# A gated cross-attention and mixture-of-experts kernel: the expert stage in 25 tiles of 256 rows and 21 tiles of 128 rows in place of 39 tiles of 256

## The chip, the cores and the metric

The kernel runs on one core of one Trainium2 chip. The metric is the device time of one execution in microseconds (us), the median over several runs. Lower is better.

## What is computed

The input x holds 4 sequences of 1024 tokens with 256 numbers each; ctx_1024 holds 77 context rows for each sequence. The reference, cut to what matters:

```python
# x: (4, 1024, 256); 16 heads of 16; 8 experts, hidden width 1024, 2 experts for each token
x = x + tanh(g_xattn) * xattn(layernorm(x), ctx, ctx)      # scores are abs(q k) / 4, softmax, then Wo
xf = layernorm(x).reshape(-1, 256)
probs = softmax(xf @ w_router)
topk_w, topk_idx = top_k(probs, 2)
weights = sum(topk_w[..., None] * one_hot(topk_idx, 8), axis=1)
h = gelu(einsum('te,ieh->tih', xf, w1) + b1)               # 256 -> 1024 in each expert
out = sum((einsum('tih,ihe->tie', h, w2) + b2) * weights[..., None], axis=1)
x = x + tanh(g_ffn) * out
```

Only the two chosen experts of a token have to be worked out. That makes 4096 x 2 = 8192 rows of expert work, spread unevenly over the 8 experts by the data.

## The kernel before, in words

**Attention stage.** Tokens go in 16 pairs of tiles (256 rows) through layer norm, attention, the router and a scatter: each token's normalised row, its 8 expert weights and its number (265 numbers in all) are written to two places of a DRAM buffer `routed`, one in the region of each chosen expert. The regions have room for all rows, so the rows of an expert lie packed from the start of its region.

**The plan.** When the counts are known, VectorE works out a table for the tiles of the expert stage: `expert_of[tile]` and `row_of[tile]` (L1307 to L1360, some 20 small dependent operations, each with its wait on the semaphore `plan`; `planned` and L1109 to L1143 did the same for the first six tiles, `EARLY_TILES`, from a count taken earlier). A count of 256 rows per tile that does not come out even leaves a partly filled tile for each expert. So there are always 8192 / 256 + 7 = 39 tiles (`MAX_TILES`, L66), whatever the data; rows beyond an expert's end are padding (`pad_rows`, weight 0), and unused tiles point at a padding region.

**Expert stage.** Each tile of 256 rows goes through five engines, which are kept in step by semaphores (`ready` waits for a count; `settled` the same with a no-op):

- SP (`load_tile`, L651) reads `row_of` and starts the DMA of 256 rows into `x_row[:, pj]`, two buffers.
- PE (`turn_tile`, L1533) turns the rows with four transposes of 128x128 float32 into the bank `X_T`; ACT (`high_rows`) writes the float16 high part `x_hi`, DVE (`low_rows`, L1154) the rest `x_lo`.
- PE (`first_layer`, L1514): for each of 8 chunks of 128 hidden units and each of the 2 chunks of 128 inputs three products, w1_hi x_hi, w1_hi x_lo and w1_lo x_hi. So that is 48 matmuls, with 128x128 weights from w1 and 256 columns of rows moving. Two chunks share one of four PSUM banks (`HID_BANKS`).
- ACT (`gelu`, L872) applies bias and gelu, a chunk at a time; DVE (`split_hidden`, L1145) splits the result into h_hi and h_lo, two chunks at a time.
- PE (`second_layer`, L1542): for both halves of 128 rows and 8 chunks three products, again 48 matmuls. Here the hidden rows (128x128) are the loaded weights and 256 columns of w2 move.
- DVE (`finish_rows`, L1159) adds the bias and multiplies by weight and gate; POOL (L763) adds the 128 rows of each half to `out` with an indirect DMA. A tile's first one waits until those of the tile before have landed (L770). POOL also copies the weights and row numbers aside (`copy_meta`, L756), once the `added` count of two tiles before is there.

The order on PE is, for tile j: first layer of j, transposes of j+1, second layer of j-1 (`step`, L1555). `tile_pipeline` (L475) writes the first and last tiles out and runs the middle ones (8 to 35) in a loop. The expert of a tile is a number in a register, so `expert` (L594) loads it from the table at each use (L600), and the address of each weight slice is worked out in PE's own instruction queue, ahead of the matmul:

```python
                            for w, x in ((k.w1_hi, x_hi), (k.w1_hi, x_lo), (k.w1_lo, x_hi)):
                                mm = pe.matmul(
                                    H[:, q, c % PER * SLOTS:(c % PER + 1) * SLOTS],
                                    w[:, bass.ds(e, 1), i, c * P:(c + 1) * P].rearrange("p a n -> p (a n)"),
```

PE touches e with each (chunk, input chunk) of the first layer and each chunk of the second one. Waits on a semaphore stand in the same queue.

Of the kernel before, what the change touches and what calls it, by code (L numbers as in the profile page):

```python
# [22 lines left out]
F16 = mybir.dt.float16  # L23
BF16 = mybir.dt.bfloat16
I32 = mybir.dt.int32
# [40 lines left out]
MAX_TILES = TOKENS * 2 // SLOTS + E - 1  # L66
EARLY_TILES = 6
OWN_META = (2, 3, 4, 5)
EARLY_PAIRS = 10
LATE_TILES = MAX_TILES - EARLY_TILES  # L70
assert EARLY_PAIRS * 4 * 128 > (EARLY_TILES - 1) * SLOTS + E * (SLOTS - 1)
FULL_TILES = MAX_TILES - 2 * (E - 1)
# [68 lines left out]
def setup_phase(nc, t, k):  # L141

    banks = k.banks
    with ExitStack() as ctx:
# [17 lines left out]
        iota_j = sb("iota_j", [P, MAX_TILES + 1], I32)  # L162
# [26 lines left out]
        with nc.Block() as block:  # L189
# [75 lines left out]
            def _(pool):  # L265
# [20 lines left out]
                pool.iota(iota_j[:], pattern=[[1, MAX_TILES + 1]], base=0, channel_multiplier=0).then_inc(made, 1)  # L286
# [178 lines left out]

LOOP_TILES = range(8, MAX_TILES - 3 - (MAX_TILES - 3) % 2)
FULL_TILES_LOADED = 10
assert EARLY_TILES < LOOP_TILES.start and EARLY_TILES <= FULL_TILES_LOADED <= min(FULL_TILES, LOOP_TILES.start + 2)


def tile_exists(tile):
    return not isinstance(tile, int) or 0 <= tile < MAX_TILES

# [11 lines left out]

def main_phase(nc, t, k, out, routed):
# [5 lines left out]
    NT = LATE_TILES + 1  # L492
# [8 lines left out]
    with ExitStack() as ctx:  # L501
# [3 lines left out]
        def sem(name):  # L505
# [37 lines left out]
        packed_row, run_of, skipped, late, row_f, expert_f = (  # L543
            plan_place[:, NT * RUNS + i * NT:NT * RUNS + (i + 1) * NT] for i in range(6))
# [3 lines left out]
        early = sb("early", [P, E])  # L548
# [4 lines left out]
        hid = stage[:].rearrange("p a n -> p (a n)").rearrange("p (c n) -> p c n", c=HC)  # L553
        h_hi = prob[:].rearrange("p i n -> p (i n)").bitcast(F16)[:, 0:2 * HC * SLOTS].rearrange(
            "p (i c n) -> p i c n", i=2, c=HC)
        h_lo = k.v_area[:].bitcast(F16).rearrange("p (i c n) -> p i c n", i=2, c=HC)
# [28 lines left out]
        PLAN_OPS = 21  # L585
# [3 lines left out]
        added = [sem(f"added{i}") for i in range(2)]  # L589
        xt_done, x_hi_sb, x_lo_sb = sem("xt_done"), sem("x_hi_sb"), sem("x_lo_sb")  # L590
# [14 lines left out]
        def meta_of(j, pj):  # L605

            if isinstance(j, int) and j in OWN_META:
                return meta[:, j] if j < 4 else late_meta[:, j - 4]
            return meta[:, pj]

# [19 lines left out]
        with nc.Block() as block:  # L630
            @block.sync
            def _(sp):
# [22 lines left out]

                def step(m, par):
                    j, mj, pj = item(m, par, 2)
                    if isinstance(j, int) and j == FULL_TILES_LOADED:
                        sp.wait_ge(k.pads, 16 * (E + 1))
                    if tile_exists(j):  # L660
                        load_tile(j, pj)
                    if isinstance(j, int) and j == EARLY_TILES:
# [31 lines left out]
                for i in range(2):  # L694
                    sp.wait_ge(added[i], 16 * SB * ((MAX_TILES + 1 - i) // 2))

            @block.gpsimd
            def _(pool):
# [63 lines left out]

                def step(m, par):  # L763
                    j, mj, pj = item(m, par, -2)
                    if tile_exists(j):
# [5 lines left out]
                        for b in range(SB):  # L771
# [3 lines left out]
                                y[:, pj, b], None, compute_op=ALU.add).then_inc(added[pj], 16)  # L775
                    j, mj, pj = item(m, par, 0)
                    if tile_exists(j) and (not isinstance(j, int) or j not in OWN_META):
                        copy_meta(j, mj, pj)

# [20 lines left out]
            def _(act):  # L800
# [85 lines left out]

                def step(m, par):
# [5 lines left out]
                    j, mj, pj = item(m, par, 1)  # L893
                    if tile_exists(j):
                        high_rows(j)
# [74 lines left out]
            def _(dve):  # L970
# [203 lines left out]

                def step(m, par):
# [4 lines left out]
                    j, mj, pj = item(m, par, 1)  # L1180
                    if tile_exists(j):
                        low_rows(j)
                    j, mj, pj = item(m, par, -1)
                    if tile_exists(j):
                        finish_rows(j, mj, pj)

# [123 lines left out]
                dve.wait_ge(plan_consts, 1)  # L1310
                dve.tensor_scalar(packed_row[:], k.tile_no[:, 0:NT], float(SLOTS), run_base[:, 0:1], ALU.mult, ALU.add)\
                    .then_inc(plan_consts, 1)
                dve.memset(run_base[:, RUNS:RUNS + 1], float(E * REGION)).then_inc(plan_consts, 1)
                dve.wait_ge(count_ps, 1)
                dve.tensor_tensor(k.pad_at[:], ROUTE[:, 0:E], k.region_of[:], ALU.add).then_inc(plan, 1)
                dve.tensor_copy(count_i[:, 0], ROUTE[:, 0:E]).then_inc(plan, 1)
                dve.tensor_scalar(count_i[:, 1], ROUTE[:, 0:E], float(SLOTS - 1), None, ALU.add).then_inc(plan, 1)
                done(3)

                dve.tensor_scalar(tiles_i[:], count_i[:], SLOTS.bit_length() - 1, None, ALU.logical_shift_right)\  # L1320
                    .then_inc(plan, 1)
                done(4)
                dve.tensor_copy(run_length[:], tiles_i[:]).then_inc(plan, 1)
                done(5)
                dve.wait_ge(plan_consts, 3)
                dve.tensor_tensor(run_length[:, 1], run_length[:, 1], run_length[:, 0], ALU.subtract).then_inc(plan, 1)
                dve.scalar_tensor_tensor(run_base[:, E:RUNS], run_length[:, 0], float(SLOTS), k.region_of[:],
                                         ALU.mult, ALU.add).then_inc(plan, 1)
                done(7)
                dve.tensor_tensor(run_length[:, 0], run_length[:, 0], early[:], ALU.subtract).then_inc(plan, 1)  # L1330
                dve.tensor_tensor(jump[:], run_base[:, 1:RUNS + 1], run_base[:, 0:RUNS], ALU.subtract)\
                    .then_inc(plan, 1)
                done(8)
                dve.tensor_tensor(upto_runs, upto, lengths.unsqueeze(1).to_broadcast([P, RUNS, RUNS]), ALU.mult)\
                    .then_inc(plan, 1)
                done(10)
# [454 lines left out]
```

## Time and profile before

| | us |
|---|---|
| median of 3 runs (709.91 to 711.79) | 710.87 |
| the profiled execution's own time | 711.22 |
| its span in the profile | 709.5 |
| matmuls (PE) busy | 686.8 (97%) |
| weight loads (PEld) busy, beside the matmuls | 621.6 (88%) |
| VectorE (DVE) busy | 478.6 (67%) |
| ScalarE (ACT) busy | 339.3 (48%) |
| GpSimd (POOL) busy | 315.4 (44%) |

The profiled execution took 1.7 us beyond its span, which is time ahead of the first and behind the last instruction. The attention stage lasts until about 280 us, and the expert stage to the end. A matmul's record (273 ns for 256 columns) holds its way through the array, so matmuls overlap: the pace is the distance of starts. PEldq is PE's instruction queue, which works out addresses, loads registers and waits.

### The profile page before, as it was taken

What the parts mean: (1) busy time and instruction counts of PE and PEld (TensorE: products, weight loads), DVE (VectorE), ACT (ScalarE), POOL (GpSimd) and SP (SyncE); (2) the same over time, 40 slices, a digit from 0 to 9 for tenths busy, and PEclk for the clock granted to TensorE, in tenths of its full rate; (3) what the DMA queues carried; (4) which work ended last, traced back from release to release, by engine and by line L of the source; (5) the groups of instructions that cost most, each with busy time, mean ns of one, the idle gap of its engine ahead of it and who ended that gap; (6) DMA issues with size and microseconds to landing.
All of it is one profiled execution on the core that took longest, in us unless ns stands there. A gap on an engine that the chain in (4) does not pass through costs nothing.

```text
span 709.5 us, 21524 instructions
## 1 busy us (share of the span) xinstructions
PE 686.8 (97%) x6793; PEld 621.6 (88%) x6794; DVE 478.6 (67%) x1246; ACT 339.3 (48%) x708; POOL 315.4 (44%) x420
## 2 busy tenths in 40 slices
PE   8899999999999998999999999999999999999992
PEld 6799999999999987898998998998989989889882
DVE  5787888887887857786575565665755656557551
ACT  4677777777677655233243342332433423324330
POOL 7324676777765547825232232332322323323233
PEclk9999999999999999999999999999999999999997
DMA  5244545455444533373332332333323323233222
GB/s 192 64 135 135 163 138 175 149 159 178 155 131 156 167 128 120 94 175 44 55 47 45 48 52 51 45 52 54 45 45 51 49 51 45 46 59 45 48 31 30
DMA packets 53091, 64.78 MB, mean 91 GB/s; under 512 B 4577, under 2 KB 48743, under 8 KB 52903
## 3 DMA queue, kind: packets, MB, share of 16 engines
q1 hardware_dynamic: 38479, 44.89, 20.9%
q0 software_dynamic: 14448, 19.06, 16.3%
q8 instruction: 37, 0.61, 0.4%
q14 instruction: 23, 0.19, 0.1%
q10 hardware_dynamic: 104, 0.04, 0.0%
HBM read 38.34 MB, written 25.54 MB: 90 GB/s over the span
## 4 chain that ended last, share of the span: by engine, by line
PE 58%; POOL 2%; issue 1%; DMA 1%; DVE 0%; POOLq 0%; DVEq 0%
PE banks L1548 28%; PE banks L1526 27%; PE banks L1538 2%; POOL routed L752 1%; DMA out_dram<-prob_t,meta 1%; POOL l_exp L735 0%; POOLq L630 0%; POOL out_dram L773 0%; POOL rstd L708 0%; DVE prob_t L1167 0%; DVE prob_t L1171 0%; POOL neg_mean L705 0%; DVE best_i L1041 0%; POOL meta L761 0%; DVE chosen L1050 0%
## 5 line engine op out<-in xcount | busy, mean ns | idle before, releaser
L876 ACT ACTIVATE stage<-banks,bias_t 128x256 f32<-128x256 f32 x312 | 130.8, 470 | 267.6 <-PE banks L1526 267.6
L1526 PE MATMUL banks<-xn_t,w_hi 128*128 128x256 f16 x1248 | 207.9, 274 | 0.7 <-DVE xn_t L1156 0.6
L773 POOL DMA_INDIRECT out_dram<-prob_t,meta x74 | 117.9, 1593 | 186.1 <-DVE prob_t L1171 164.9
L1526 PE MATMUL banks<-xn_t,w_lo 128*128 128x256 f16 x624 | 170.6, 273 | 0.0
L1548 PE MATMUL banks<-w_hi,v_area 128*128 x624 | 170.1, 273 | 0.0
L1548 PE MATMUL banks<-w_hi,prob 128*128 x624 | 170.1, 273 | 0.0
L1548 PE MATMUL banks<-w_lo,prob 128*128 x624 | 170.1, 273 | 0.0
L1526 PEld LDWEIGHTS banks<-xn_t,w_hi 128*128 x1248 | 122.3, 98 | 15.5 <-issue 1.2
L1151 DVE TENSOR_TENSOR v_area<-stage,prob 128x512 f16<-128x512 f32 x156 | 108.5, 695 | 5.4
L1167 DVE SCALAR_TENSOR_TENSOR prob_t<-banks,arena 128x256 f32<-128x256 f32 x78 | 32.8, 421 | 114.1 <-PE banks L1548 112.0
L752 POOL DMA_INDIRECT routed<-row,pos x64 | 69.8, 1091 | 27.9 <-issue 14.3
L1149 DVE CAST prob<-stage 128x512 f16<-128x512 f32 x156 | 67.2, 431 | 21.7 <-ACT stage L876 19.0
L1457 PEld LDWEIGHTS banks<-v_area,prob_t 128*128 128x128 f32 x640 | 73.9, 192 | 4.3 <-DVE attn L1000 0.7
L1457 PE MATMUL banks<-v_area,prob_t 128*128 128x34 f32 (+1 forms) x640 | 77.2, 277 | 0.3 <-DVE attn L1000 0.3
L1526 PEld LDWEIGHTS banks<-xn_t,w_lo 128*128 x624 | 61.3, 98 | 7.3
L1548 PEld LDWEIGHTS banks<-w_hi,v_area 128*128 128x128 f16 x624 | 61.0, 98 | 7.1
L1548 PEld LDWEIGHTS banks<-w_lo,prob 128*128 128x128 f16 x624 | 61.0, 98 | 7.1
L1548 PEld LDWEIGHTS banks<-w_hi,prob 128*128 128x128 f16 x624 | 61.0, 98 | 6.7
L981 DVE TENSOR_REDUCE top<-prob 128x16 f32<-128x1232 f32 x32 | 45.9, 1434 | 26.7 <-ACT prob L804 26.7
L1438 PE MATMUL banks<-ident,prob 128*128 128x128 f32 x320 | 51.2, 274 | 0.1
L832 ACT ACTIVATE prob_t<-banks 128x512 f32<-128x512 f32 (+1 forms) x96 | 45.6, 537 | 6.5 <-PE banks L1443 4.9
L761 POOL COPY meta<-x_row 128x18 f32<-128x18 f32 x37 | 7.6, 205 | 79.4 <-DMA out_dram<-prob_t,meta 74.7
(218 smaller groups left out, 991.0 us busy)
## 6 DMA issues: line engine op xcount, KB each, us to landing
stage<-in_L_ffn_w_dram SPq DMA_DIRECT2D x32, 512.0 KB, 4.0
x_row<-routed SPq DMA_DIRECT2D x39, 265.0 KB, 2.8
x_in<-in_x_dram SPq DMA_DIRECT2D x16, 256.0 KB, 3.4
x_res<-in_x_dram SPq DMA_DIRECT2D x16, 256.0 KB, 3.8
out_dram<-x_res SPq DMA_DIRECT2D x16, 256.0 KB, 2.7
routed<-pad_rows SPq DMA_DIRECT2D x9, 265.0 KB, 3.5
out_dram<-prob_t,meta POOLq DMA_INDIRECT x74, 3.8
routed<-row,pos POOLq DMA_INDIRECT x64, 2.8
```

What stands on the lines that cost most here:

```text
L752: pool.indirect_dma_start(routed[:, :], bass.IndirectOffsetOnAxis(ap=pos[:, held, tile, choice:choice + 1], axis=0), row[:, held, tile], N ...
L773: pool.indirect_dma_start(out[:, :], bass.IndirectOffsetOnAxis(ap=meta_of(j, pj)[:, b, E:E + 1].bitcast(U32), axis=0), y[:, pj, b], None, ...
L832: act.activation(prob_t[:, first:first + n, :].rearrange("p c n -> p (c n)"), T[:, g, 0:n * P], ACT.Exp, scale=DH ** -0.5).then_inc(pt_sb, 1)
L876: ins = act.activation(hid[:, c], H[:, q, c % PER * SLOTS:(c % PER + 1) * SLOTS], ACT.Gelu_apprx_tanh, bias=k.bias_t[:, bass.ds(e * HC + c ...
L981: dve.tensor_reduce(top_part(i, 0), prob[:, i % 2, 0:SCORES].rearrange("p (h k) -> p h k", k=KEYS), AX.X, ALU.max).then_inc(top_sb, 1)
L1149: dve.tensor_copy(h_hi[:, pj, part], hid[:, part]).then_inc(h_hi_sb, 1)
L1151: dve.tensor_tensor(h_lo[:, pj, part], hid[:, part], h_hi[:, pj, part], ALU.subtract)\
L1167: dve.scalar_tensor_tensor(y[:, pj, b], Y[pj][:, b * D:(b + 1) * D], 1.0 / W_SCALE, b2_b[:, bass.ds(e, 1), :].rearrange("p a d -> p (a d)" ...
L1438: pe.matmul(T[:, g, c * P:(c + 1) * P], prob[:, i % 2, (first + c) * P:(first + c + 1) * P], k.ident[:], is_transpose=True, start=(c == 0) ...
L1457: mm = pe.matmul(V[:, first * VW:(first + n) * VW], prob_t[:, c, :], k.v_rows[:, b, c, 0:n * VW], start=(c == 0), stop=(c == PCH - 1), ski ...
L1526: mm = pe.matmul(H[:, q, c % PER * SLOTS:(c % PER + 1) * SLOTS], w[:, bass.ds(e, 1), i, c * P:(c + 1) * P].rearrange("p a n -> p (a n)"), ...
L1548: mm = pe.matmul(Y[pj][:, b * D:(b + 1) * D], h[:, pj, c, b * P:(b + 1) * P], w[:, bass.ds(e, 1), c, :].rearrange("p a n -> p (a n)"), sta ...
```

## The change

The expert stage has two sorts of tiles. The first 25 (`FULL_TILES`, 32 - 7) have 256 rows and go on as before, with the loop over tiles 8 to 21. Behind them come 21 tiles of 128 rows (`SMALL_TILES`, (8192 - 25 * 256) / 128 + 7), written out. The plan takes full tiles only from whole 256 rows of an expert and shares the rest out to small ones. For a small tile the row DMA has 128 rows with four buffers, there are two transposes, and one scatter. On PE the two layers alternate: chunk c of tile j's first layer (6 matmuls of 128 columns), then chunk c of tile j-1's second layer (3 matmuls of 256 columns), with the transposes of j+1 after chunk 3. The plan has 31 operations on the semaphore `plan` in place of 21, and a table of 40 late tiles in place of 34.

```diff
 SLOTS = 256
 SB = SLOTS // P
-MAX_TILES = TOKENS * 2 // SLOTS + E - 1
+FULL_TILES = TOKENS * 2 // SLOTS - (E - 1)
+SMALL_TILES = (TOKENS * 2 - FULL_TILES * SLOTS) // P + E - 1
+MAX_TILES = FULL_TILES + SMALL_TILES
...
-LOOP_TILES = range(8, MAX_TILES - 3 - (MAX_TILES - 3) % 2)
+LOOP_TILES = range(8, FULL_TILES - 3 - (FULL_TILES - 3) % 2)
...
-    NT = LATE_TILES + 1
+    NT = LATE_TILES
...
-        PLAN_OPS = 21
+        PLAN_OPS = 31
...
+                def load_small(t):
+                    before = t - 2 if t < FULL_TILES + 2 else t - 4
+                    p, h, b = small_turn(t)
...
+                    ready(sp, xt_done, before)
+                    ready(sp, meta_sb, before)
+                    at = sp.value_load(k.row_of[0:1, t:t + 1], min_val=0, max_val=E * REGION)
+                    sp.dma_start(k.x_row[:, p, b], routed[bass.ds(at, P), :]).then_inc(small_ld[p][b], 16)
...
+                def scatter_small(t):
+                    p, h, b = small_turn(t)
+                    if t == FULL_TILES:
+                        ready(pool, added[0], FULL_TILES // 2, 16 * SB)
+                    else:
+                        ready(pool, small_added[1 - p], small_turn(t - 1)[1], 16)
+                    settled(pool, y_sb, t, SB)
+                    pool.indirect_dma_start(
+                        out[:, :], bass.IndirectOffsetOnAxis(ap=small_meta(t)[:, E:E + 1].bitcast(U32), axis=0),
+                        y[:, p, 0], None, compute_op=ALU.add).then_inc(small_added[p], 16)
...
+                def gelu_small(t, e, q):
+                    ready(act, hid_ps, t, HID_BANKS, q + 1)
+                    ready(act, h_lo_sb, t - 1, HID_BANKS, q + 1)
+                    for c in range(PER):
+                        ins = act.activation(small_part(hid_flat, q)[:, c * P:(c + 1) * P], H[:, q, c * P:(c + 1) * P],
...
+                    elif small_exists(j):
+                        e = expert(act, j)
+                        for q in range(HID_BANKS):
+                            gelu_small(j, e, q)
+                            if q == 1 and small_exists(j + 1):
+                                high_small_rows(j + 1)
...
+                def finish_small_rows(t):
+                    p, h, b = small_turn(t)
+                    e = expert(dve, t)
+                    ready(dve, y_ps, t)
+                    if t < FULL_TILES + 2:
+                        dve.wait_ge(added[p], 16 * SB * len(range(p, FULL_TILES, 2)))
+                    else:
+                        dve.wait_ge(small_added[p], 16 * h)
...
+                        for q in range(HID_BANKS):
+                            split_small_hidden(j, q)
+                            if q == 1 and small_exists(j + 1):
+                                low_small_rows(j + 1)
...
+                dve.tensor_tensor(upto_eight, upto[:, 0:E, 0:E], run_length[:, 0].unsqueeze(1).to_broadcast([P, E, E]),
+                                  ALU.mult).then_inc(plan, 1)
+                done(6)
+                dve.tensor_reduce(run_end[:, 0:E], upto_eight, AX.X, ALU.add).then_inc(plan, 1)
+                done(7)
+                dve.tensor_scalar(run_end[:, 0:E], run_end[:, 0:E], float(LATE_FULL), None, ALU.min).then_inc(plan, 1)
...
+                def first_small(t, e, c):
+                    q = c // PER
+                    if c == 0:
+                        ready(pe, x_lo_sb, t)
+                    if c % PER == 0:
+                        ready(pe, hid_sb, t - 1, HID_BANKS, q + 1)
+                    hi, lo = (x[t % 2].rearrange("p (i n) -> p i n", i=KC) for x in (small_x_hi, small_x_lo))
+                    n = 0
+                    for i in range(KC):
+                        for w, x in ((k.w1_hi, hi), (k.w1_hi, lo), (k.w1_lo, hi)):
+                            mm = pe.matmul(H[:, q, c % PER * P:(c % PER + 1) * P],
+                                           w[:, bass.ds(e, 1), i, c * P:(c + 1) * P].rearrange("p a n -> p (a n)"),
+                                           x[:, i], start=(n == 0), stop=(n == 3 * KC - 1))
+                            n += 1
...
+                def turn_small(t):
+                    p, h, b = small_turn(t)
+                    ready(pe, small_ld[p][b], h // 2, 16)
+                    ready(pe, x_lo_sb, t - 1)
+                    for i in range(KC):
+                        mm = pe.transpose(X_T[:, i * P:(i + 1) * P], x_row[:, p, b, i * P:(i + 1) * P], k.ident[:])
+                    mm.then_inc(xt_done, 1)
+
+                def second_small(t, e, c):
+                    p = t % 2
+                    if c == 0:
+                        ready(pe, y_bias, t - 2, SB)
+                    if c % PER == 0:
+                        ready(pe, h_lo_sb, t, HID_BANKS, c // PER + 1)
+                    for n, (h, w) in enumerate(((small_h_hi, k.w2_hi), (small_h_hi, k.w2_lo), (small_h_lo, k.w2_hi))):
+                        mm = pe.matmul(Y[p][:, 0:D], h[p][:, c * P:(c + 1) * P],
+                                       w[:, bass.ds(e, 1), c, :].rearrange("p a n -> p (a n)"),
+                                       start=(c == 0 and n == 0), stop=(c == HC - 1 and n == 2))
...
+                    elif isinstance(j, int):
+                        if small_exists(j):
+                            e = expert(pe, j)
+                        if small_exists(j - 1):
+                            e_before = expert(pe, j - 1)
+                        for c in range(HC):
+                            if small_exists(j):
+                                first_small(j, e, c)
+                            if small_exists(j - 1):
+                                second_small(j - 1, e_before, c)
+                            if c == 3 and small_exists(j + 1):
+                                turn_small(j + 1)
```

## Rows read from the trace of the kernel before

**Rows 1.** Page: busy time of PE, and its granted clock in 40 slices.

```profile
PE 686.8 (97%) x6793; PEld 621.6 (88%) x6794; DVE 478.6 (67%) x1246; ACT 339.3 (48%) x708; POOL 315.4 (44%) x420
...
PEclk9999999999999999999999999999999999999997
```

**Rows 2.** Chain that ended last, from 639.97 us: start, us, what.

```profile
664.53 0.44 PE banks L1538 x4
664.97 5.24 PE banks L1548 x48
670.21 5.24 PE banks L1526 x48
...
686.37 5.25 PE banks L1548 x48
...
695.37 3.83 DMA out_dram<-prob_t,meta
...
701.57 1.86 POOLq L630
```

**Rows 3.** PE's queue by line: ns min/median/max, first to last start.

```profile
L1526 PEldq FUSED_REGOPS  x12: 46/46/46, 494.4 to 497.2; - x12
...
L1548 PEldq FUSED_REGOPS  x8: 46/46/46, 587.2 to 588.9; - x8
```

**Rows 4.** The same view around loads of a tile's expert.

```profile
L600 PEldq TENSOR_LOAD <-expert_of x1: 300/300/300, 684.3 to 684.3; - x1
...
L105 PEldq EVENT_SEMAPHORE  x1: 51/51/51, 684.9 to 684.9; - x1
...
L1548 PEldq FUSED_REGOPS  x8: 46/46/46, 685.0 to 686.8; - x8
...
L600 PEldq TENSOR_LOAD <-expert_of x4: 298/299/312, 673.8 to 689.5; - x4
```

**Rows 5.** The same view of L1548 and L1526, 309.6 to 691.7 us (35 tiles).

```profile
L1548 PEldq FUSED_REGOPS  x286: 46/46/46, 314.4 to 691.5; - x143
...
L1526 PEldq FUSED_REGOPS  x556: 46/46/46, 309.8 to 683.9; - x186
```

**Rows 6.** Timeline, attention stage: start, us, engine, instructions.

```profile
150.67 0.39 PE L1443 MATMUL banks<-top_t,spread_top 128*128 128x128 bf16 x4
...
150.56 0.32 PEld L1443 LDWEIGHTS banks<-top_t,spread_top 128*128 128x128 bf16 x4
```

**Rows 7.** Page, part 5 and 6: ACT, DVE and the scatters of the expert stage.

```profile
L876 ACT ACTIVATE stage<-banks,bias_t 128x256 f32<-128x256 f32 x312 | 130.8, 470 | 267.6 <-PE banks L1526 267.6
...
L1151 DVE TENSOR_TENSOR v_area<-stage,prob 128x512 f16<-128x512 f32 x156 | 108.5, 695 | 5.4
...
L1149 DVE CAST prob<-stage 128x512 f16<-128x512 f32 x156 | 67.2, 431 | 21.7 <-ACT stage L876 19.0
...
out_dram<-prob_t,meta POOLq DMA_INDIRECT x74, 3.8
```

**Rows 8.** Timeline of DVE and POOL from 690 us.

```profile
692.32 0.41 DVE L1171 TENSOR_SCALAR prob_t<-prob_t,meta,gates 128x256 f32<-128x256 f32 x1
...
693.50 1.57 POOL L773 DMA_INDIRECT out_dram<-prob_t,meta  x1 [4.16 <-DVE prob_t L1171]
...
701.87 1.55 POOL L773 DMA_INDIRECT out_dram<-prob_t,meta  x1 [0.30 <-issue]
```

**Rows 9.** Timeline of DVE and PEld, 298 to 321 us (the plan).

```profile
301.20 0.72 DVE L1341 TENSOR_TENSOR x_in<-tile_no,run_end 128x544 f32<-128x544 f32 x1
...
305.56 0.69 DVE L1156 TENSOR_TENSOR xn_t<-banks,xn_t 128x512 f16<-128x512 f32 x1 [0.92 <-ACT xn_t L885]
...
319.88 0.68 DVE L1156 TENSOR_TENSOR xn_t<-banks,xn_t 128x512 f16<-128x512 f32 x1
...
320.70 0.11 PEld L1526 LDWEIGHTS banks<-xn_t,w_hi 128*128 x2 [0.32 <-issue]
```

**Rows 10.** Windows: us, PE, PEld, DVE, ACT, POOL busy (x), PEclk, DMA share, GB/s.

```profile
140.00:170.00 30.00, 30.00 (x344) 28.01 (x343) 24.74 (x85) 22.57 (x42) 21.90 (x35) 1.00 0.51 161
```

More of the change, by code:

```diff
@@ L463, in _, with small_exists, small_turn @@
                     mm.then_inc(k.v_done, 1)
-LOOP_TILES = range(8, MAX_TILES - 3 - (MAX_TILES - 3) % 2)
-FULL_TILES_LOADED = 10
-assert EARLY_TILES < LOOP_TILES.start and EARLY_TILES <= FULL_TILES_LOADED <= min(FULL_TILES, LOOP_TILES.start + 2)
+LOOP_TILES = range(8, FULL_TILES - 3 - (FULL_TILES - 3) % 2)
+assert EARLY_TILES < LOOP_TILES.start and LATE_FULL >= 0 and FULL_TILES % 2 == 1
 def tile_exists(tile):
-    return not isinstance(tile, int) or 0 <= tile < MAX_TILES
+    return not isinstance(tile, int) or 0 <= tile < FULL_TILES
+def small_exists(tile):
+    return isinstance(tile, int) and FULL_TILES <= tile < MAX_TILES
+def small_turn(tile):
+    h = (tile - FULL_TILES) // 2
+    return tile % 2, h, h % 2
 def tile_pipeline(eng, step, first):
@@ L541, in main_phase @@
         past = plan_place[:, 0:NT * RUNS].rearrange("p (n r) -> p n r", r=RUNS)
-        packed_row, run_of, skipped, late, row_f, expert_f = (
-            plan_place[:, NT * RUNS + i * NT:NT * RUNS + (i + 1) * NT] for i in range(6))
+        packed_row, run_of, skipped, late, row_f, expert_f, halved = (
+            plan_place[:, NT * RUNS + i * NT:NT * RUNS + (i + 1) * NT] for i in range(7))
         upto, upto_runs = (x_norm[:, i].rearrange("p (n r) -> p n r", r=RUNS) for i in range(2))
@@ L552, in main_phase @@
             "p (c n) -> p c n", c=KC) for i in range(2))
[L553 to L556, printed above, removed]
+        hid_flat = stage[:].rearrange("p a n -> p (a n)")
+        hid = hid_flat.rearrange("p (c n) -> p c n", c=HC)
+        h_hi_flat = prob[:].rearrange("p i n -> p (i n)").bitcast(F16)
+        h_lo_flat = k.v_area[:].bitcast(F16)
+        h_hi, h_lo = (h[:, 0:2 * HC * SLOTS].rearrange("p (i c n) -> p i c n", i=2, c=HC) for h in (h_hi_flat, h_lo_flat))
+        small_h_hi, small_h_lo = (
+            [h[:, i * HC * SLOTS:i * HC * SLOTS + HC * P] for i in range(2)] for h in (h_hi_flat, h_lo_flat))
+        small_x_hi, small_x_lo = (
+            [x.rearrange("p c n -> p (c n)")[:, i * KC * P:(i + 1) * KC * P] for i in range(2)] for x in (x_hi, x_lo))
         y = prob_t[:].rearrange("p c n -> p (c n)")[:, 0:2 * SB * D].rearrange("p (i b d) -> p i b d", i=2, b=SB)
@@ L589, in main_phase @@
         added = [sem(f"added{i}") for i in range(2)]
+        small_ld = [[sem(f"small_ld{i}{b}") for b in range(2)] for i in range(2)]
+        small_added = [sem(f"small_added{i}") for i in range(2)]
         xt_done, x_hi_sb, x_lo_sb = sem("xt_done"), sem("x_hi_sb"), sem("x_lo_sb")
@@ L609, in meta_of, with small_meta @@
             return meta[:, pj]
+        def small_meta(tile):
+            p, _, b = small_turn(tile)
+            return meta[:, p + 2 * (1 - b), 0]
         def chunk_parts(turn):
@@ L1318, in _ @@
                 done(3)
-                dve.tensor_scalar(tiles_i[:], count_i[:], SLOTS.bit_length() - 1, None, ALU.logical_shift_right)\
-                    .then_inc(plan, 1)
[L1322 to L1327, printed above, removed]
+                dve.tensor_copy(run_length[:, 0], tiles_i[:, 0]).then_inc(plan, 1)
@@ new lines, in _ @@
+                done(8)
+                dve.tensor_copy(run_length[:, 0, 0:1], run_end[:, 0:1]).then_inc(plan, 1)
+                dve.tensor_tensor(run_length[:, 0, 1:E], run_end[:, 1:E], run_end[:, 0:E - 1], ALU.subtract)\
+                    .then_inc(plan, 1)
+                done(10)
+                dve.tensor_tensor(taken[:], run_length[:, 0], early[:], ALU.add).then_inc(plan, 1)
+                done(11)
+                dve.scalar_tensor_tensor(l_left[:], taken[:], -float(SLOTS), ROUTE[:, 0:E], ALU.mult, ALU.add)\
+                    .then_inc(plan, 1)
@@ new lines, in _ @@
+                dve.tensor_tensor(upto_eight, upto[:, 0:E, 0:E], run_length[:, 1].unsqueeze(1).to_broadcast([P, E, E]),
+                                  ALU.mult).then_inc(plan, 1)
+                dve.scalar_tensor_tensor(skip[:, E:RUNS], run_length[:, 1], -float(P), jump[:, E:RUNS], ALU.mult, ALU.add)\
+                    .then_inc(plan, 1)
+                done(19)
+                dve.tensor_reduce(run_end[:, E:RUNS], upto_eight, AX.X, ALU.add).then_inc(plan, 1)
+                done(21)
```

148 lines of the change are left out of this document (107 added, 41 removed).

## The prediction

> **What bounds the kernel now.** Read the page first: PE is busy for 97% of the span at full clock [rows 1]. Next comes the chain of waits. Through the expert stage it runs on PE alone: 0.44 us for four transposes, 5.24 us for 48 matmuls of one layer, 5.24 us for 48 of the other [rows 2]. A step is 10.92 us, and a matmul of 256 columns starts every 5.24 / 48 = 0.109 us. ScalarE, VectorE and the scatters have gaps beside that.
>
> The third view is PE's own instruction queue, and it matters most. It works out the addresses of the weight slices, in pairs of one FUSED_REGOPS and one ALU_OP, and a pair serves three matmuls. When the queue is not held up, 12 pairs of the first layer start within 2.8 us, with two waits of 0.1 us among them: (2.8 - 0.2) / 11 = 0.236 us a pair. 8 pairs of the second layer start within 1.7 us, 0.243 us each [rows 3]. I take 0.237. With 256 columns three matmuls last 0.327 us, so the queue stays ahead and its time is hidden. With 128 columns that cover goes.
>
> **What goes.** Steps 25 to 38 are replaced. Step 38 has no transposes, so from the end of step 24 (call it t) to the end of step 38 they take 14 x 10.92 - 0.44 = 152.4 us, up to 691.6 us [rows 2]. The span's end is 17.9 us later. Together it is 170.3 us from t, which is near 539.2 us.
>
> **What a small step streams on PE.** First layer: 48 matmuls of 128 columns. The attention stage has such matmuls with new 16-bit weights for each: four take 0.39 us with the last one's 0.219 us, so they start every (0.39 - 0.22) / 3 = 0.056 us [rows 6]. 48 x 0.056 = 2.7 us. Second layer: 24 x 0.109 = 2.6 us. Two transposes: 0.2 us. The sum is 5.5 us, half of a full step. 21 of them would be worth 10.5 full steps, and 3.5 steps or 38 us would be saved, if PE only streamed.
>
> **What a small step costs in PE's queue.** A full tile has 16 pairs in the first layer (556 in 35 tiles) and only 8 in the second (286 in 36): its second half of rows uses the same addresses again [rows 5]. A small tile needs as many, since it goes through all of both weights: 24 pairs x 0.237 = 5.69 us. To this come the loads of the expert from the table. From such a load's start (684.3) to the next instruction (684.9) it is 0.6 us, and over four of them 0.65 us is the best value [rows 4]. A small step has two, for tile j and once more for j-1: 1.30 us. A wait that stands alone takes 0.1 us (684.9 to 685.0) [rows 4]; where two waits meet, one stands alone: in the first layer, the second layer and the transposes, 0.32 us. The transposes' own dispatch I put at 0.05 us. The sum is 7.36 us, 1.8 us more than PE streams. So I expect the small steps to run at 7.35 us, at the pace of the queue. The alternation by chunks helps only in part: for a chunk the queue needs 3 x 0.237 = 0.71 us and PE 6 x 0.056 + 3 x 0.109 = 0.66 us.
>
> What is unsure is mainly the transposes' part: I have no view of it with a free queue. From below it is 0; from above it is another 0.3 us, since the queue was held up for so long about a full tile's four. I stay near the lower end, for a small tile has two. With the rounding of a pair (0.236 to 0.243) a step lies between 7.2 and 7.7 us.
>
> **The sum.** Step 25 has a small first layer alone and then the full second layer of tile 24. The queue gets to the load of the expert some 2.1 us before PE is done with the step ahead (last load 689.5 [rows 4], PE until 691.6 [rows 2]), so PE streams 2.9 us at once, waits until 3.4 us for the next load and addresses, and then streams 5.24 us: to t + 8.6. The queue is free at t + 6.5. Twenty steps (26 to 45) of 7.35 are 147.0 us; PE trails the last address by some 0.3 us. Tile 44's second layer ends at t + 153.8.
>
> The tail from there: gelu, split and expert load of tile 45 stand before tile 44's finish on VectorE. A gelu takes 0.47, a cast 0.43 and a subtraction 0.69 us at full size [rows 7]; from half of each I put the last scaling at 2.1 us. From a scaling's start to its scatter it is 1.2 us (692.3 to 693.5) [rows 8], to its landing 3.8 [rows 2, 7]; the last scatter starts 0.8 us later, as it waits for that landing, and the span ends 7.6 us after its start (701.9 to 709.5) [rows 8]. That is 15.5 us, and the end is at t + 169.3. Before it was t + 170.3. So 1.0 us is saved here.
>
> The plan: ten more dependent operations of some 0.2 us each, smaller ones in place of two of 0.42 us, and four passes over 640 numbers in place of 544, each of which took 0.72 us [rows 9] and will take 0.12 more. I count 2.2 us until the table is done. The next operation had waited 0.92 us for ScalarE, which absorbs as much. The rest, 1.3 us, goes on: VectorE works with hardly a gap up to the rows of tile 5 (319.88), for which PE already waited (0.32 us before the weight load at 320.70) [rows 9]. PE would be 1.3 us late there, and nothing gives this back.
>
> Costed at nothing: the row DMAs (128 rows, four buffers, a step of lead); ScalarE, 8 shorter gelus of at most 0.47 us and a copy, about 3.4 us in a step of 7.35; VectorE, four splits of half of 1.12 us and a finish, about 4.2 us; POOL, whose scatters wait for one another: 3.8 us to landing and 0.8 to the next start are 4.6 us, for which 5.5 would do too. If a step fell to 4.6 us, the scatters would be next. PE's waits on x_lo and h_lo come 1 us or more after these are written, and the wait on `pads` is long met.
>
> Net: -1.0 + 1.3 = +0.3 us. The profiled execution took 711.2 us, and the median is 0.35 us less: 710.87 + 0.3 gives **711.2 us**. About 0.3% (2.1 us) is what a measurement of this kernel can tell from no change; twenty steps of 0.1 us are as much. So the sign of a small effect is open.
>
> **A rule that speaks against the change.** Each weight load's record lasts 98 ns, but four of them start within 0.32 - 0.10 = 0.22 us and do not hold up the matmuls at 0.056 us [rows 6]. The Trainium skill, page "TensorE: Matmul & The Clock Gate", section "LDWEIGHTS (loading the stationary operand)", gives a load as its columns / 1.2, which is 107 ns for 128 columns; by it a small step would be 48 x 0.107 + 2.6 + 0.3 = 8.0 us, 13 us more over twenty steps. The same page's part on fast weight load says that 16-bit weights of 128 columns load about twice as fast. The first of these rules is the third rival below; that runs in the attention stage are of four only is what leaves it alive.
>
> **The rivals.** (1) PE streams without the queue holding it, because the compiled code has fewer address operations or they are hidden in another way. Steps of 5.5 us then: t + 8.6 + 110.6 + 15.5 = 134.7, 35.6 us less than before, with the plan 34.3: 676.6 us. For it speaks that the queue never held PE so far; against it the constant pace of [rows 3]. Chance 0.13. (2) In between, for instance one expert load or some of the addresses saved, steps of 6.4 us: 692 us. Chance 0.06. (3) Weight loads that hold up the small matmuls: if in runs of six a load has to end before the next can start, a step is 48 x 0.098 + 2.6 + 0.3 = 7.6 us on PE itself, and the queue's lead of 2.1 us and 2.0 us of step 25 are lost too: 5 + 2.1 + 2.0 less the 0.3 of trailing, with +0.3 some 9 us, 720 us. It decides from 94 ns a load on, for there 48 loads and the rest reach 7.35 us. Against it stand [rows 6]. Chance 0.08. (4) The queue needs more than my list: 7.65 us a step for transposes and waits that it stops at: 6 us more, 717 us. Chance 0.11. (5) My sum within 0.25 us a step: 706 to 716 us, 0.62. The clock should not fall: it stayed at 1.00, the 2.4 GHz level, through 140 to 170 us with shorter and sparser matmuls [rows 10].
>
> **The numbers.** Forecast 711.2. The range 700 to 722 leaves out (1), half of (2) and a little above. Of the 0.62 of my case, 0.17 are faster by over 0.3%, 0.31 within and 0.14 slower. With (1) and (2) faster is 0.36; with 0.03 of (4) the same is 0.34; slower 0.30.
>
> **What to look for after.** Small steps (starts of the first chunk) 7.35 us apart, from the end of tile 24 on, with PE's gaps at the expert loads and pairs of addresses 0.237 us apart without hold-ups; first-layer matmuls 0.056 us apart within a run of three and with gaps between; 24 pairs and two loads a step; 21 steps over about 155 us; PE's wait before tile 5 about 1.3 us longer. I am wrong if the steps are near 5.5 us, if the small matmuls start 0.1 us apart, if pairs are fewer than 24, or if waits for the scatters show on VectorE.

## The result and the profile after

The changed kernel takes 720.7 us (median of 4 runs, 718.6 to 721.5) where the kernel before took 710.4 us beside it: a ratio of 1.014, with a 95% interval of 1.011 to 1.016. It is slower by 10 us. 711.2 us had been forecast, with a range of 700 to 722. So the result lies in the range, but only 1.3 us below its upper end, and the likeliest case was too friendly: a ratio of about 1.00 was forecast, and a third of the chances stood for each sign.

The page after, with the lines that answer to [rows 1] and [rows 7]:

```profile
PE 670.6 (93%) x6947; PEld 596.3 (83%) x6948; DVE 471.7 (66%) x1307; ACT 344.5 (48%) x771; POOL 305.9 (43%) x420
...
PE   7899999999999998999999999999999888888883
...
PEclk9999999999999999999999999999999999999997
...
L951 ACT ACTIVATE stage<-banks,bias_t 128x128 f32<-128x128 f32 x168 | 52.7, 364 | 107.9 <-PE banks L1713 107.0
...
L1713 PE MATMUL banks<-xn_t,w_hi 128*128 128x128 f16 x672 | 77.0, 220 | 22.2 <-ACT stage L951 22.2
...
out_dram<-prob_t,meta POOLq DMA_INDIRECT x67, 3.8
```

PE has 16 us less to do, and the time is longer. The granted clock stayed at 1.00 in the stage of the small tiles (the column after POOL in the windows below). The eight slices of PE before the last are at 8 and not 9: PE idles in every small step. The windows show how much (PE, PEld, DVE, ACT, POOL busy, clock, DMA share, GB/s), first after, over the steps 25 to 45, then before, over the steps 25 to 38:

```profile
541.50:703.10 161.60, 138.24 (x1577) 113.85 (x1574) 85.60 (x232) 57.88 (x187) 41.01 (x44) 1.00 0.24 37
```

```profile
539.20:691.60 152.40, 152.40 (x1399) 137.19 (x1397) 92.64 (x181) 53.30 (x125) 47.15 (x42) 1.00 0.30 47
```

PE is busy for 138 of 161.6 us. The timeline shows where the rest lies: start, us, matmuls, with PE's idle time in brackets, at the end of one small step and the start of the next.

```profile
602.64 0.27 PE L1735 MATMUL banks<-w_lo,prob 128*128 x1
602.75 0.27 PE L1735 MATMUL banks<-w_hi,v_area 128*128 x1
604.26 0.28 PE L1713 MATMUL banks<-xn_t,w_hi 128*128 128x128 f16 x2 [1.24 <-ACT stage L951]
604.38 0.22 PE L1713 MATMUL banks<-xn_t,w_lo 128*128 128x128 f16 x1
604.50 0.28 PE L1713 MATMUL banks<-xn_t,w_hi 128*128 128x128 f16 x2
604.62 0.22 PE L1713 MATMUL banks<-xn_t,w_lo 128*128 128x128 f16 x1
604.84 0.28 PE L1735 MATMUL banks<-w_hi,prob 128*128 x1
```

Two things are to be seen. No matmul starts between 602.75 and 604.26, and the profile names ScalarE as the releaser. And inside the step three matmuls of the first layer need 0.24 us (604.26 to 604.50), though they can start 0.056 us apart. PE's own queue, over that step (L1713 is the first layer of a small tile, L1735 its second, L624 the load of the expert, L107 the waits):

```profile
L624 PEldq TENSOR_LOAD <-expert_of x2: 303/306/309, 602.7 to 603.3; - x2
...
L107 PEldq EVENT_SEMAPHORE  x3: 51/51/51, 604.0 to 607.2; - x3
...
L1713 PEldq FUSED_REGOPS  x16: 46/46/51, 604.2 to 609.8; - x16
...
L1735 PEldq FUSED_REGOPS  x8: 46/46/46, 604.7 to 610.2; - x8
```

The two table loads take 602.7 to 604.0, which is the hole in PE's work. Behind them come 16 + 8 pairs of address operations and three lone waits until 610.4, where the next load starts. This is the list of the prediction, item by item. If it is what sets the step, ScalarE has nothing to do with the hole, whatever the releaser says; the experiments check that.

How far apart the steps are is read from the transposes. Tiles 27 to 45 have two each, so 38 starts span 18 steps and 0.1 us:

```profile
L1725 PE MATMUL banks<-ident,x_row x38: 271/272/273, 553.4 to 692.5; 128*128 128x128 f32 x38
```

(692.5 - 553.4 - 0.1) / 18 = 7.72 us a step, where 7.35 had been forecast. At the start of the stage PE waits for the rows of tile 5, as [rows 9] had it with 0.32 us:

```profile
323.23 0.11 PEld L1674 LDWEIGHTS banks<-xn_t,w_hi 128*128 x2 [1.70 <-issue]
```

The span's 9.0 us come together like this. Step 24 ends 2.3 us later (541.5 against 539.2): 1.4 us are the longer wait for tile 5, and the rest was there before: PE's first matmul for the expert stage, the transposes of tile 0, starts at 251.8 us against 250.6, behind an attention stage that the change does not touch. (Two transposes fewer in step 24 give 0.2 us back.) The small stage takes 161.6 us in place of 152.4, 9.2 more. The tail takes 15.4 us in place of 17.9, 2.5 less. 2.3 + 9.2 - 2.5 = 9.0.

### The profile page after: what moved, and what is told of

Its sections match the earlier page's. It is cut to its first block, busy times and chain, and to the rows that moved or that the text cites. A ratio compares the mean times of both kernels' runs of the same rounds, so it can differ in the third digit from the quotient of the medians.

```text
span 718.5 us, 22083 instructions
## 1 busy us (share of the span) xinstructions
PE 670.6 (93%) x6947; PEld 596.3 (83%) x6948; DVE 471.7 (66%) x1307; ACT 344.5 (48%) x771; POOL 305.9 (43%) x420
## 4 chain that ended last, share of the span: by engine, by line
PE 48%; issue 5%; DVE 4%; POOL 3%; ACTq 1%; ACT 1%; DMA 1%; DVEq 0%; POOLq 0%
PE banks L1696 15%; PE banks L1674 15%; PE banks L1713 8%; PE banks L1735 8%; POOL routed L792 2%; PE banks L1686 1%; ACT stage L951 1%; POOL l_exp L775 1%; ACTq L624 1%; DVE prob L1232 1%; PE banks L1725 1%; DMA out_dram<-prob_t,meta 1%; DVE prob_t L1250 0%; DVE prob_t L1254 0%; DVE xn_t L1239 0%
## 5 line engine op out<-in xcount | busy, mean ns | idle before, releaser
L936 ACT ACTIVATE stage<-banks,bias_t 128x256 f32<-128x256 f32 x200 | 84.1, 471 | 170.3 <-PE banks L1674 170.2
L1674 PE MATMUL banks<-xn_t,w_hi 128*128 128x256 f16 x800 | 134.2, 275 | 2.1 <-DVE xn_t L1239 2.1
L1674 PE MATMUL banks<-xn_t,w_lo 128*128 128x256 f16 x400 | 109.8, 274 | 0.0
L1696 PE MATMUL banks<-w_hi,prob 128*128 x400 | 109.0, 273 | 0.7 <-DVE v_area L1264 0.7
L1696 PE MATMUL banks<-w_hi,v_area 128*128 x400 | 109.0, 273 | 0.0
L1696 PE MATMUL banks<-w_lo,prob 128*128 x400 | 109.0, 273 | 0.0
L951 ACT ACTIVATE stage<-banks,bias_t 128x128 f32<-128x128 f32 x168 | 52.7, 364 | 107.9 <-PE banks L1713 107.0
L1713 PE MATMUL banks<-xn_t,w_hi 128*128 128x128 f16 x672 | 77.0, 220 | 22.2 <-ACT stage L951 22.2
L1713 PEld LDWEIGHTS banks<-xn_t,w_hi 128*128 x672 | 51.9, 97 | 34.0 <-issue 27.8
L1234 DVE TENSOR_TENSOR v_area<-stage,prob 128x512 f16<-128x512 f32 x100 | 69.6, 696 | 3.4
L1713 PE MATMUL banks<-xn_t,w_lo 128*128 128x128 f16 x336 | 67.3, 219 | 0.0
```

What stands on the lines that cost most here:

```text
L936: ins = act.activation(hid[:, c], H[:, q, c % PER * SLOTS:(c % PER + 1) * SLOTS], ACT.Gelu_apprx_tanh, bias=k.bias_t[:, bass.ds(e * HC + c ...
L951: ins = act.activation(small_part(hid_flat, q)[:, c * P:(c + 1) * P], H[:, q, c * P:(c + 1) * P], ACT.Gelu_apprx_tanh, bias=k.bias_t[:, ba ...
L1234: dve.tensor_tensor(h_lo[:, pj, part], hid[:, part], h_hi[:, pj, part], ALU.subtract)\
L1674: mm = pe.matmul(H[:, q, c % PER * SLOTS:(c % PER + 1) * SLOTS], w[:, bass.ds(e, 1), i, c * P:(c + 1) * P].rearrange("p a n -> p (a n)"), ...
L1696: mm = pe.matmul(Y[pj][:, b * D:(b + 1) * D], h[:, pj, c, b * P:(b + 1) * P], w[:, bass.ds(e, 1), c, :].rearrange("p a n -> p (a n)"), sta ...
L1713: mm = pe.matmul(H[:, q, c % PER * P:(c % PER + 1) * P], w[:, bass.ds(e, 1), i, c * P:(c + 1) * P].rearrange("p a n -> p (a n)"), x[:, i], ...
```

## The experiments

Two theories stood against mine. Mine (Q): a small step lasts as long as PE's own instruction queue needs. Rival W: the weight loads hold up the small matmuls. Rival D: PE waits for ScalarE and VectorE, as the profile's releaser says. The first four experiments ran on one chip and the second four on another, each time beside the kernel before, with medians of 713.3 us (19 runs) and 713.0 us (7 runs); ratios are to these. Where only one run was made, the steps in its trace carry the argument and not its time: the steps are steady from one profile to another (7.72 us in two kernels with the same small steps, 6.59 us in two others), and the start of the kernel is not.

**One load of the expert in place of two.** The register of tile j is kept for its second layer, one step later.

```diff
-                        if small_exists(j):
-                            e = expert(pe, j)
                         if small_exists(j - 1):
-                            e_before = expert(pe, j - 1)
+                            e_before = held[0]
+                        if small_exists(j):
+                            e = held[0] = expert(pe, j)
```

> The one change: in the small steps PE's queue loads the expert from the table once and not twice (the register of tile j is kept for tile j's second layer one step later). Theory Q (a small step lasts as long as PE's own instruction queue needs: 24 pairs of address operations, two table loads, three lone waits, measured 7.72 us): each step loses one load of 0.65 to 0.70 us, so steps of 7.05 us, 13 to 14 us less over twenty steps, about 707 us. Rival W (the 128-column matmuls are held up by their weight loads, so PE itself sets the step): no change, 720 us. Rival D (PE waits for results of ScalarE and VectorE at the start of each step, as the chain of waits suggests with its 'issue' and ACT pieces there): no change or under 3 us, since those results come no earlier.

706.0 us (10 runs), ratio 0.991 (0.988 to 0.993): faster than the kernel before. Its transposes, and the second layer's address operations in one step:

```profile
L1725 PE MATMUL banks<-ident,x_row x38: 271/272/300, 553.3 to 678.2; 128*128 128x128 f32 x38
...
L1735 PEldq ALU_OP  x16: 32/32/32, 591.9 to 597.4; - x16
```

A step is 6.93 us, 0.79 less. Both rivals had at most 3 us less in all, and here the same matmuls, weight loads, gelus and splits run in shorter steps. The gain is some 0.1 us more than a load. The second row says why: with the register kept, the eight FUSED_REGOPS of the second layer have become ALU_OPs, and a pair of these takes 0.225 us in place of 0.237. Over 18 steps of each trace, all pairs together take 5.95 us a step in place of 6.06, and the loads 0.65 in place of 1.31.

**Fixed addresses in the second layer.** Small tiles use expert 0's w2 whatever the table says, so the choice of the expert is left out there. Both loads stay.

```diff
-                                       w[:, bass.ds(e, 1), c, :].rearrange("p a n -> p (a n)"),
+                                       w[:, 0, c, :],
```

> Left out: the choice of the expert in the second layer of the small tiles; they all use expert 0's w2, at fixed addresses. Both table loads stay. Theory Q: 8 pairs of address operations go, at 0.24 to 0.25 us each, so steps of 7.72 - 2.0 = 5.75 us, 40 us less over twenty steps, about 681 us. Rival W: the matmuls and weight loads are all still there, so no change, 720 us. Rival D: no change either.

686.7 us (one run). Steps of 5.94 us:

```profile
L1725 PE MATMUL banks<-ident,x_row x38: 272/272/273, 553.9 to 660.9; 128*128 128x128 f32 x38
```

The same matmuls with the same data sizes, and 1.78 us less a step for 8 pairs; 2.0 were expected, and 681 us for the kernel. The step is now near what PE streams, which the next run gives as 5.64. That the queue alone no longer sets it would explain the missing 0.2 us; no run shows it.

**Fixed addresses in both layers.** The same for w1 in the small tiles: expert 0 throughout, no address operation left.

```diff
-                                           w[:, bass.ds(e, 1), i, c * P:(c + 1) * P].rearrange("p a n -> p (a n)"),
+                                           w[:, 0, i, c * P:(c + 1) * P],
```

> Left out: the choice of the expert in both layers of the small tiles (expert 0's weights at fixed addresses). Both table loads stay, no address operation is left. Theory Q: the queue needs some 1.8 us and the dispatch of 74 pairs, so PE's streaming sets the step: 5.5 us, from 48 x 0.056 + 24 x 0.109 + 0.2, 44 us less, about 676 us, and weight loads of 98 ns start 0.056 us apart in runs of six. Rival W: small matmuls at least 0.098 us apart, 7.6 us a step, 718 us. If steps lie between (6 us and more) although the queue is free, dispatch or the scatters' chain (4.6 us) adds something that I have not listed.

679.5 us (one run). The lines view, PE's transposes:

```profile
L1725 PE MATMUL banks<-ident,x_row x38: 272/273/273, 551.6 to 653.2; 128*128 128x128 f32 x38
```

The windows view of the small stage, with the columns as above:

```profile
541.50:660.00 118.50, 118.22 (x1548) 108.95 (x1546) 81.70 (x229) 57.04 (x184) 39.26 (x43) 1.00 0.30 48
```

The timeline of PE, matmuls of the first layer and the first of the second (start, us):

```profile
599.88 0.27 PE L1713 MATMUL banks<-xn_t,w_hi 128*128 128x128 f16 x2
599.99 0.22 PE L1713 MATMUL banks<-xn_t,w_lo 128*128 128x128 f16 x1
600.04 0.27 PE L1713 MATMUL banks<-xn_t,w_hi 128*128 128x128 f16 x2
600.15 0.22 PE L1713 MATMUL banks<-xn_t,w_lo 128*128 128x128 f16 x1
600.21 0.27 PE L1735 MATMUL banks<-w_hi,prob 128*128 128x256 f16 x1
```

And the timeline of the weight loads beside them:

```profile
599.94 0.10 PEld L1713 LDWEIGHTS banks<-xn_t,w_lo 128*128 128x128 f16 x1
599.99 0.15 PEld L1713 LDWEIGHTS banks<-xn_t,w_hi 128*128 128x128 f16 x2
600.10 0.10 PEld L1713 LDWEIGHTS banks<-xn_t,w_lo 128*128 128x128 f16 x1
```

PE is busy for all of the small stage, at 5.64 us a step. Six small matmuls start within 599.88 to 600.21, which is 0.055 us each, and two weight loads are done in 0.15 us. So weight loads of 98 ns do not hold up runs of six. The two table loads, still there, leave no hole once the queue is ahead. With the same gelus and splits the step has fallen by 2.1 us, so rival D is out too. This is what 21 small tiles would be worth if their addresses were free: some 34 us under the kernel before, by one run.

**No alternation.** First all chunks of one layer, then all of the other.

```diff
                         for c in range(HC):
                             if small_exists(j):
                                 first_small(j, e, c)
-                            if small_exists(j - 1):
-                                second_small(j - 1, e_before, c)
                             if c == 3 and small_exists(j + 1):
                                 turn_small(j + 1)
+                        for c in range(HC):
+                            if small_exists(j - 1):
+                                second_small(j - 1, e_before, c)
```

> The one change: the two layers of a small step do not alternate by chunks; the 8 chunks of the first layer of tile j (with the transposes of j+1 after the fourth) come first, then the 8 chunks of the second layer of tile j-1. Theory Q: the queue has the same instructions, so a step stays at 7.7 us and the time at 720 us, within 2 us; PE is ahead in the first part and behind in the second. If the alternation hides work of the queue (what its order is good for: 0.71 us of queue beside 0.66 us of PE per chunk), the steps would be up to 0.7 us longer without it: 8 x 0.09 us more PE time behind the queue in the second part, 734 us at most.

721.3 us (10 runs), ratio 1.011 (1.008 to 1.013). Steps of 7.7 us, as with the alternation:

```profile
L1725 PE MATMUL banks<-ident,x_row x38: 272/286/303, 554.8 to 693.6; 128*128 128x128 f32 x38
```

The queue has the same instructions in another order, and the step is the same. The prediction had the alternation help in part; while the queue sets the pace it does nothing. With a shorter queue it was not tried. This run is also the nearest thing to the changed kernel on the chip of the first four: 721.3 us there, to be held against 706.0.

**The plan's first part earlier.** The changed kernel with the plan's constants and first seven operations moved to where VectorE waits for the last router shares.

```diff
+                def done(part):
+                    dve.wait_ge(plan, part)
...
+                dve.tensor_reduce(run_end[:, 0:E], upto_eight, AX.X, ALU.add).then_inc(plan, 1)
                 shares(PAIRS - 1)
```

> The changed kernel with one thing moved: the first seven operations of the plan (up to the sum over the early full tiles) and its constants stand before VectorE's wait for the last router shares, where VectorE sits idle for 2.2 us, and not behind the third tile's split. My theory of the start: the longer plan holds up the rows of tile 5, for which PE waits 1.7 us here and 0.3 us in the kernel before. Moved, some 2 us less stand in that stretch, so PE's gap before tile 5's first layer falls from 1.7 to 0.1 to 0.4 us, and the time by about 1.4 us. Rival: the gap comes from somewhere else in VectorE's order (the finishing of tiles 1 and 2); then it stays at 1.5 to 1.7 us.

721.1 us (one run). The gap before tile 5 is gone; the timeline of PE there has no idle time left:

```profile
323.45 0.27 PE L1696 MATMUL banks<-w_hi,v_area 128*128 x1
323.58 0.39 PE L1674 MATMUL banks<-xn_t,w_hi 128*128 128x256 f16 x2
```

That is what the theory of the start says. The time of this one run shows no gain where 1.4 us were expected: tile 5 starts at 323.6 us here and at 323.2 us in the changed kernel. This execution was already 0.7 us later at PE's first matmul for the expert stage, and short waits of PE before tiles 2 and 3, which the changed kernel's profile does not have, made that 1.9 us at tile 3; at tile 5 only 0.4 us of it are left. The combined kernel below has the same move without these waits. Alone this run says nothing about the time.

**One load and no lone waits.** A wait that another one implies goes: the hidden bank at chunk 0, `y_bias`, and `x_lo` at the transposes.

```diff
-                    if c % PER == 0:
+                    elif c % PER == 0:
                         ready(pe, hid_sb, t - 1, HID_BANKS, q + 1)
...
-                    if c == 0:
-                        ready(pe, y_bias, t - 2, SB)
...
-                    ready(pe, x_lo_sb, t - 1)
```

> On top of the one table load: the three lone waits of a small step that another wait already implies are gone (the hidden bank at chunk 0, implied by x_lo; y_bias, implied by h_lo; x_lo again at the transposes). Theory Q: each was an instruction of 0.106 us in PE's queue, so steps of 6.93 - 0.32 = 6.6 us, 6.4 us less than with one load: about 700 us on a chip where one load alone gives 706. Theory that only loads matter because PE is drained at a step's start: waits in the middle of a step cost nothing, 0.1 to 0.2 us a step at most, 703 us or more.

698.0 us (4 runs), ratio 0.979 (0.976 to 0.982), with steps of 6.59 us:

```profile
L1724 PE MATMUL banks<-ident,x_row x38: 271/272/273, 553.8 to 672.5; 128*128 128x128 f32 x38
```

Three instructions of 0.106 us, hold-ups left out, have gone and the step is 0.34 us shorter. The records of the three lone waits of the changed kernel last 51 ns each (L107 above), so none of them was held up by what it waited for: they cost their place in the queue.

**All three.** The register kept, the implied waits dropped and the plan's first part earlier, in one kernel; its edits are those of the three diffs above.

> One load, no lone waits, and the plan's first part moved. Theory Q and my theory of the start together: steps of 6.6 us and no gap before tile 5, 1.4 us less than e7_fewer_waits, about 698 us, 2% under the kernel before on the same chip.

696.7 us (4 runs), ratio 0.978 (0.974 to 0.982). The steps are those of the run before, and no gap is left at the start. It is 1.3 us under that run, as expected, but the two intervals overlap, so the gain in time is not shown. It is 2.2% under the kernel before, where the changed kernel was 1.4% over the one beside it.

**An extra load in the full tiles of the kernel before.** A second load of the expert that nothing uses.

```diff
                     if tile_exists(j):
                         e = expert(pe, j)
+                        expert(pe, j)
```

> The kernel before with one more load of the expert from the table in PE's queue for each full tile, which nothing uses. Theory Q: in a full step the queue needs 24 pairs, three loads now, and waits, some 8.5 us beside 10.92 us of matmuls, so the same 0.65 us that costs a small step its full length costs nothing here: steps stay at 10.92 us, the time within noise of the kernel before (at most 1 us more). If a table load stops PE by itself (because it waits until PE has drained, say), each step is 0.65 us longer, 20 us more in all.

719.6 us (one run), where at most 1 us over 713.0 was expected. The transposes of 17 full tiles, 16 steps and 0.3 us, with the load and in the kernel before:

```profile
L1538 PE MATMUL banks<-ident,x_row x68: 272/273/273, 507.8 to 684.1; 128*128 128x128 f32 x68
```

```profile
L1538 PE MATMUL banks<-ident,x_row x68: 272/273/273, 500.6 to 675.6; 128*128 128x128 f32 x68
```

A step is 11.00 us in place of 10.92, so 0.08 us of the 0.65 us show: the matmuls of a full tile hide the load, but not to the last bit. Over 33 steps that is about 2.6 us. Against the profiled execution of the kernel before, whose span is 8.4 us shorter, 4.2 us were there at PE's first matmul for the expert stage (254.8 us against 250.6), ahead of any extra load. Another 1.9 us came up by tile 5, mostly in waits before tiles 2 and 3. The run with the plan moved has waits at the same two places without an extra load, so whether the load has a part in them a single run does not tell.

## Why the prediction was right, and what it missed

**What bounds it.** Right. The queue, hidden behind 256-column matmuls, comes out with 128 columns. One load, the dropped waits and the two kernels with fixed addresses show it: steps follow the queue's instructions while the matmuls stay the same.

**PE's streaming.** 5.5 us forecast, 5.64 measured with the queue out of the way. So, by 0.14 us more in each of 21 steps, some 35 of the 38 us of saved streaming were real, and they were lost to the queue.

**The queue's list.** The items and their number were right: two loads, 24 pairs, three lone waits. The sum was 0.37 us too small a step, and over 20 steps 7.4 of the 9.5 us between forecast and result come from this. The mis-sized term is the price of a pair. Over 18 small steps, from one first load to the next, the starts in PE's queue give, in us a step:

| | forecast | measured |
|---|---|---|
| 24 pairs | 5.69 | 6.06 |
| two loads | 1.30 | 1.31 |
| three lone waits | 0.32 | 0.36 |
| dispatch of the transposes | 0.05 | within the others |
| sum | 7.36 | 7.73 |

A pair costs 0.252 us and not 0.237. The lower price is right for a stretch without hold-ups; what was put at nothing are the hold-ups, which come about once in 1 us and add 0.37 us a step. The price could have been had: in [rows 4] the eight pairs of one tile start within 685.0 to 686.8 us, 0.257 us each. I went by the two quiet stretches of [rows 3].

Of the rest, 1.0 us is what step 24 ended later beyond the 1.3 us forecast, 0.4 us lies in the small stage beyond its twenty steps, and about 0.9 us is the distance from the profiled span to the median: 2.2 us (720.7 to 718.5), where the forecast had taken over 1.4 us from the kernel before.

**The unsure term** was the transposes. It was the wrong place to look: nothing of them shows beyond the three items of the list, and the error lay in the best-founded term, which was multiplied by 480. A step between 7.2 and 7.7 us had been given, and 7.72 is just outside. The step is nearest to rival 4's 7.65 us (717 us), but for another reason than that rival's. The time alone could not have told the cases apart: 720.7 us is almost what rival 3, the weight loads, would have given (720 us). Another 0.07 us a step would have put it outside the range, so that it lies inside is in part luck.

**The tail.** 15.5 us forecast, 15.4 measured, with some luck: the last scaling starts 2.35 us behind the small stage (2.1 forecast), and the span ends 7.3 us after the last scatter starts (7.6 forecast).

**The plan.** PE was forecast to start tile 5 1.3 us later; the gap grew by 1.4 us. The run with the plan's first part moved closed it.

**What nobody had forecast.** Some 1 us ahead of tile 2. PE's first matmul for the expert stage starts between 250.6 and 254.8 us in the ten profiles, both ends being kernels with the same attention stage, so the executions differ by more than this there. Why is open.

**The rivals.** Rival 1 (PE streams unhindered) is what the run with fixed addresses shows as a counterfactual: 679.5 us, where 676.6 had been worked out. Rival 3 (weight loads) is out: six in a row start 0.055 us apart. (Its threshold of 94 ns a load should have read 93.) By the Trainium skill's rule of columns / 1.2 (page "TensorE: Matmul & The Clock Gate", section "LDWEIGHTS (loading the stationary operand)") a step would have been 8.0 us, an estimate; the run with all addresses fixed, at 5.64 us, disagrees. The same page of the Trainium skill says in the section "Weight-path perf modes — Fast Weight Load (FWL) and DoubleRow" that fast weight load was measured at about twice the speed. The pace agrees: one load with its matmul every 0.055 us is about half of the rule's 107 ns, though each load's record still lasts 98 ns.

**The signs.** With a likeliest case of +0.3 us and an unsure term of 2 us on each side, a third for each sign was right in form. But the corrections that I had before me, a higher price of a pair and more for the transposes, could only add. A list of instructions at their undisturbed prices is a lower bound, and the forecast should have stood above it.

## What to carry to other kernels

When tiles are made smaller, count what each one costs the engine's instruction queue (address operations, register loads, lone waits), since that does not shrink with the tile; here it is 24 pairs and two loads for 128 rows as for 256. The page does not count these instructions as busy, and it puts the resulting idle time down to whichever engine's semaphore was waited on last, so look at the queue's own instructions of a line before believing the releaser. Take the price of an instruction in the queue from long stretches, hold-ups included. Then take things out of the queue before rearranging the matmuls: keeping a register and dropping implied waits turned 1.4% slower into 2.1% faster, each against the kernel before beside it, and alternating the layers did nothing.

## What the runs showed of the hardware that I had not expected

- An address pair costs 0.237 us in undisturbed stretches and 0.252 us on average over 18 small steps. About once in 1 us the way from one address operation to the next is 0.01 to 0.15 us longer than usual. What this is stays open.
- An ALU_OP costs about 0.112 us and a FUSED_REGOPS 0.124 us of the queue, though the records say 32 and 46 ns. The duration of a record is not its price; the distance of starts is.
- Matmuls and weight loads between two address operations hardly add to the queue. By the order of the program, four stand behind a FUSED_REGOPS of the first layer and two behind one of the second, and the distance to the ALU_OP is 0.124 us in both.
- The kernel before took 710.2 to 716.6 us over the 19 runs beside the first four experiments and 710.7 to 715.7 over the 7 beside the second four, but 709.9 to 711.8 over the 4 beside the changed kernel. So a single time here is good to some 3 us.
